# A router whose weight matrix becomes the stationary operand, with its logits turned back by small transposes

## The reference

```python
h = _layernorm(x) * (1 + cb) + sb               # x: 4 x 1024 x 256, after attention
probs = softmax(h @ Wr)                         # Wr: 256 x 8 experts
topk_probs, topk_experts = top_k(probs, 2)
for e in range(8):                              # at most 1280 tokens for each expert
    vals, idx = top_k(gate_of_expert_e, 1280)
    y = y.at[idx].add(g[:, None] * (relu(h[idx] @ W1[e]) @ W2[e]))
```

## Time and profile before

| | before |
|---|---|
| median of three runs | 1213.57 us |
| profiled execution, its own time | 1209.35 us |
| its span | 1207.5 us |
| TensorE busy | 1129.0 us (93%) |
| VectorE busy | 816.3 us (68%) |
| ScalarE busy | 420.4 us (35%) |
| GpSimd busy | 544.8 us (45%) |
| mean granted TensorE clock | 0.945 of full |

### The profile page before, as it was taken

The page is one execution under the profiler, slowest core; times in us unless marked ns, Lnnn a source line. Parts: engine busy times, 40 slices in busy tenths (PEclk is TensorE's granted clock), DMA queues, the critical chain, the costliest instruction groups (busy, mean ns, idle before and its releaser), DMA issues.

```text
span 1207.5 us, 17088 instructions
## 1 busy us (share of the span) xinstructions
PE 1129.0 (93%) x5810; PEld 980.5 (81%) x5810; DVE 816.3 (68%) x1549; ACT 420.4 (35%) x762; POOL 544.8 (45%) x403
## 2 busy tenths in 40 slices
PE   8998999999999999999985558999999999999996
PEld 5877888888888888887874447989898989899996
DVE  5587999589999999998476785444444444445442
ACT  5321122323223333231572202344353434444432
POOL 3220000377777777772000032666565657565723
PEclk9998999999999999999885558999999999999998
DMA  7110022433001111102441212754444353534322
GB/s 266 36 35 12 1 45 52 137 122 97 27 31 33 33 33 33 33 22 70 140 145 37 91 55 56 201 141 88 118 85 122 79 127 87 131 67 83 57 41 26
DMA packets 73985, 93.35 MB, mean 77 GB/s; under 512 B 5924, under 2 KB 61988, under 8 KB 73944
## 3 DMA queue, kind: packets, MB, share of 16 engines
q1 hardware_dynamic: 55928, 60.96, 16.3%
q0 software_dynamic: 18016, 31.86, 13.6%
HBM read 65.29 MB, written 23.31 MB: 73 GB/s over the span
## 4 chain that ended last, share of the span: by engine, by line
PE 73%; issue 13%; DVE 7%; ACT 2%; DMA 2%; POOL 2%; SPq 0%; DVEq 0%; POOLq 0%; ACTq 0%
PE ps L1459 27%; PE ps L1600 18%; PE ps L1616 12%; PE ps L1617 6%; PE ps L1487 2%; PE ps L1370 2%; DVE arena L1155 1%; PE ps L1582 1%; DMA qkv<-in_w 1%; DVE qkv L821 1%; PE ps L1562 1%; DVE arena_rounded L821 1%; PE ps L1545 1%; PE ps L1510 1%; ACT qkv L732 1%
## 5 line engine op out<-in xcount | busy, mean ns | idle before, releaser
L1600 PE MATMUL ps<-arena_rounded,w_high 128*128 128x384 f32 (+1 forms) x768 | 210.5, 355 | 2.1 <-DVE arena_rounded L821 2.1
L580 POOL TENSOR_TENSOR kv_low<-arena,kv_high 128x512 fp32r<-128x512 f32 x128 | 185.7, 1479 | 41.1 <-ACT kv_high L632 41.1
L1459 PE MATMUL ps<-kv_high,toep_high 128*128 128x512 f32 (+1 forms) x512 | 193.1, 377 | 1.0 <-POOL kv_low L580 1.0
L1459 PE MATMUL ps<-kv_low,toep_high 128*128 128x512 f32 (+1 forms) x512 | 193.1, 377 | 0.0
L1459 PE MATMUL ps<-kv_high,toep_low 128*128 128x512 f32 (+1 forms) x512 | 192.4, 376 | 0.0
L1272 DVE SCALAR_TENSOR_TENSOR hidden_low<-ps,hidden_high 128x384 fp32r<-128x384 f32 (+1 forms) x192 | 115.6, 602 | 98.9 <-ACT hidden_high L790 98.5
L604 POOL DMA_INDIRECT out<-arena x80 | 126.3, 1579 | 103.7 <-DVE arena L821 96.0
L593 POOL DMA_INDIRECT qkv<-row_scratch,arena x80 | 82.9, 1036 | 184.0 <-DVE arena L1226 158.0
L1600 PEld LDWEIGHTS ps<-arena_rounded,w_high 128*128 128x128 f32 x768 | 139.9, 189 | 13.2 <-issue 2.5
L790 ACT ACTIVATE hidden_high<-ps 128x384 fp32r<-128x384 f32 (+1 forms) x192 | 101.3, 528 | 125.6 <-PE ps L1600 125.6
L821 DVE TENSOR_TENSOR arena<-qkv 128x512 f32 (+1 forms) x128 | 133.3, 1099 | 7.2 <-DMA qkv<-arena 7.0
(11 more groups left out here) (198 smaller groups left out, 1971.9 us busy)
## 6 DMA issues: line engine op xcount, KB each, us to landing
arena<-ssm_scratch SPq DMA_DIRECT2D x32, 320.0 KB, 3.1
qkv<-in_w SPq DMA_DIRECT2D x16, 512.0 KB, 5.2
qkv<-in_w SPq DMA_DIRECT2D x8, 1024.0 KB, 10.7
arena<-in_u SPq DMA_DIRECT2D x7, 1024.0 KB, 6.2
row_scratch<-qkv SPq DMA_DIRECT2D x4, 1056.0 KB, 4.6
qkv<-arena SPq DMA_DIRECT2D x32, 128.0 KB, 2.4
row_scratch<-arena SPq DMA_DIRECT2D x4, 1024.0 KB, 6.4
out<-qkv SPq DMA_DIRECT2D x4, 1024.0 KB, 9.3
```

The source lines that it names most:

```text
L580: nc.gpsimd.tensor_tensor(kv_parts[s][1][:, quarter], kv_flat[s][:, quarter], kv_parts[s][0][:, quarter].bitcast(F32), ALU.subtract).then_ ...
L1459: last = mm(ps[:, 4 * s + g, (lo - 2 * g) * B * 64:BANK], toep_parts[s][a][:, o * P:(o + 1) * P], kv_parts[s][x][:, src], start=n == 0 and ...
L1600: last = mm(ps[:, f % 4, 0:width], w1_parts[q][a][:, dc * F + f * P:dc * F + (f + 1) * P], xeT_parts[x][dc][:, 0:width], start=dc == 0 and ...
```

## The change

The operands of the router are exchanged. `wr_sb` (128 features x 8 experts) is the stationary operand and the turned rows move, 512 tokens in each matmul, so a batch takes 4 matmuls, each writing 8 partitions x 512 tokens. The router now waits until all four pieces of `h2T` are there, where it waited for two and then for the other two. ScalarE copies the two halves into `logits_turned` (8 partitions x 1024) with `logits_out(b)`, which stands ahead of `normalize(b+1)`. TensorE turns them back with `logits_back(b)`, eight transposes of 8 x 128 to 128 x 8, which wait for both copies; from there VectorE reads them as before. logits_back(0) and logits_back(1) stand in the middle of attention_out(2) and attention_out(3), logits_back(2) ahead of router(3), logits_back(3) behind it.

```diff
-LOGIT_BANK = (2, 2, 0, 1)
+LOGIT_BANKS = ((2, 3), (2, 3), (0, 1), (4, 5))
...
+            def logits_out(b):
+                for half in range(2):
+                    act.wait_ge(turned_psum, 2 * b + half + 1)
+                    copy(logits_turned[0:E, half * BANK:(half + 1) * BANK],
+                         ps[0:E, LOGIT_BANKS[b][half], :]).then_inc(turned_copied, 1)
...
                 if b + 2 < B:
                     y_turned(b + 2)
+                logits_out(b)
                 if b + 1 < B:
                     normalize(b + 1)
...
                 for tb in range(TB):
+                    if tb == TB // 2 and b >= 2:
+                        logits_back(b - 2)
                     for cc in range(DC):
...
             def router(b):
+                pe.wait_ge(h2T_ready, 4 * b + 4)
+                if b == B - 1:
+                    pe.wait_ge(x2_ready, B)
+                for half in range(2):
+                    for cc in range(DC):
+                        last = mm(ps[0:E, LOGIT_BANKS[b][half], :], wr_sb[:, cc, :], h2T[b][:, cc, half * BANK:(half + 1) * BANK],
+                                  start=cc == 0, stop=cc == DC - 1)
+                    last.then_inc(turned_psum, 1)
+
+            def logits_back(b):
+                pe.wait_ge(turned_copied, 2 * b + 2)
                 for tb in range(TB):
-                    if tb % 4 == 0:
-                        pe.wait_ge(h2T_ready, 4 * b + tb // 2 + 2)
-                    for cc in range(DC):
-                        last = mm(ps[:, LOGIT_BANK[b], tb * E:(tb + 1) * E], h2T[b][:, cc, tb * P:(tb + 1) * P], wr_sb[:, cc, :],
-                                  start=cc == 0, stop=cc == DC - 1)
+                    last = transpose(ps[:, LOGIT_BANKS[b][0], tb * E:(tb + 1) * E], logits_turned[0:E, tb * P:(tb + 1) * P],
+                                     ident[0:E, 0:E])
                 last.then_inc(logit_psum, 1)
...
+                if b == B - 1:
+                    logits_back(b - 1)
                 router(b)
                 if b + 2 < B:
                     attention_out(b + 2)
+            logits_back(B - 1)
```

More of the change, by code:

```diff
@@ L207, in adaln_block @@
         ones_l = region(T0 + 1536, 256)
+        logits_turned = region(T0, 2 * BANK)
         junk = [region(T0 + start, 256) for start in (1792, 3072, 3328)]
@@ L313, in adaln_block @@
             sem(n) for n in ("w_high", "w_low", "xeT_high", "xeT_low", "hid_high", "hid_low"))
+        turned_psum, turned_copied = sem("turned_psum"), sem("turned_copied")
         waited, table_in, gates_out, rows_out, x2_out = (
@@ L1086, in centre_logits @@
                 dve.wait_ge(logit_psum, b + 1)
-                nc.vector.tensor_copy(row, ps[:, LOGIT_BANK[b], 0:TB * E].rearrange("p (t e) -> p t e", t=TB)).then_inc(logit_ready, 1)
+                nc.vector.tensor_copy(row, ps[:, LOGIT_BANKS[b][0], 0:TB * E].rearrange("p (t e) -> p t e", t=TB)).then_inc(logit_ready, 1)
                 dve.wait_ge(logit_ready, b + 1)
```

## The result

| | before | changed |
|---|---|---|
| median | 1213.05 us (9 runs, 1209.51 to 1213.73) | 1219.84 us (9 runs, 1217.11 to 1223.14) |
| profiled execution, its own time | 1209.35 us | 1220.16 us |
| its span | 1207.5 us | 1218.4 us |
| router(0) to the gates' turn, in the trace | 57.4 us (590.43 to 647.81) | 65.4 us (592.76 to 658.21) |
| start to router(0) | 590.4 us | 592.8 us |

The changed kernel is slower by 0.63%: the ratio is 1.0063 with an interval of 1.0051 to 1.0075, or 6.8 us between the medians. The stage of the router is 8.1 us longer. The 2.3 us ahead of it fall on identical instructions. From here on "the stage" is the time from the first router record to the gates' turn; where times of two kernels are compared, both are counted from router(0).

What follows compares the result with a forecast made beforehand. Bound: TensorE up to 621.8 us, then a latency chain through ScalarE and VectorE to the gates' turn at 647.81. +0.6, +1.1 and +5.5 make +7.2, with clock weighed +8: 1221.6 us on 1213.57; range 1216.5 to 1225.5.

Steps and rivals of the forecast that it cites:

- the sum: Delay at the exponential of batch 2: +0.6, +1.1 more and +5.5 more make +7.2 us.
- the clock weighed in: Half clock in part of router(2) would add 1.4 us; half of that weighed in gives +8.
- Step 1: Batch 0: TensorE gains 2.9 us, the clock staying full through router(0) and attention_out(2).
- Step 2: Batch 1: copies waiting for router(1) stand ahead of normalize(2) on ScalarE; its square root comes 0.6 us later.
- Step 3: Batch 2: the 1.28 us table load behind router(2)'s copy is no longer hidden; the square root comes 1.7 us late.
- Step 4: Batch 3: logits_out(3) makes the exponential of batch 2 wait for router(3), taken as 4.67 us; exponential 7.2 us later.
- The range: Whole time: 1216.5 us (+5.4 less 2 us between runs) to 1225.5 us (between +11 and +12.8).
- Rival of full clock throughout: TensorE holds full clock also in batch 3, router(3) takes 3.44 us: +5.4, 1219.0 us; chance 0.18.
- Rival of the clock lost as before: Routers run at half clock as before: up to +12.8, priced at +11, 1224.6 us; chance 0.17.
- Rival of a faster kernel: ScalarE's copies and table loads find cover, so the clock alone counts: -4.1, 1209.5 us; chance 0.05.
- the forecast's sign of 2 us: Sign of being wrong: a search or expert phase whose length changes by more than 2 us.

Runs made afterwards that it cites:

- the repeated run: The changed kernel measured once more, nothing altered, beside the kernel with early table loads; 1219.92 us, ratio 1.0068 to the kernel before.
- The filled kernel: The changed kernel plus five float32 matmuls of 512 columns, results unused, on TensorE ahead of h2_transposes(3); 1219.51 us, ratio 1.0057 to the kernel before.
- the best kernel: Against the kernel before: new form for batches 0 and 1, copies behind normalize(1) and normalize(2), logits_back(1) at three quarters of attention_out(3); 1208.35 us, ratio 0.9968.

## Why the prediction was right

The forecast was 1221.6 us, 8.0 over the 1213.57 of the three runs then shown; measured were 1219.84 and 6.8 over the 1213.05 of nine. The stage, which is what the steps speak of, became 8.1 us longer, where the sum says 7.2, and 8 with the clock weighed in. The mechanism was right at each step; that 8 meets 8.1 so closely is luck, since the 0.8 were put in for a half clock in router(2), which did not come, and were made up by router(3) and by a slower batch 0.

- Step 1 held, with a gain of 2.5 us where 2.9 was said. The clock stayed full, router(0) left TensorE after 3.53 us (592.76 to 596.29; 3.44 expected), logits_back took 0.59 (0.5 taken), and h2_transposes(1) stood at 11.3 us where 11.0 was expected.
- Step 2 held, larger: the square root of batch 2 is 22.2 us behind router(0), before 21.1. The loss is 1.0 us where 0.6 was expected, since router(1) started at 16.6 us instead of 16.2: the halves of attention_out(2) took 3.65 and 3.55 us, where 3.5 was taken, and router(0), logits_back(0) and the transposes ahead of router(1) 0.1 more each. The wait of h2_transposes(2) for VectorE is there, 1.83 us.
- Step 3 held. The table load follows the copy (630.11, 630.72, 632.01), and the square root of batch 3 is 2.1 us late, 1.7 expected; of these 0.4 are step 2's. No drain is seen here either: the load starts 0.6 us behind the start of a copy of 0.59 us, ends at 632.00, and the square root starts at 632.01. By the Trainium skill ("ScalarE: Activation LUTs", section on what ACT_TABLE_LOAD costs) a switch costs 1.38 us of drain besides the load. The measurement decides: there is no room for it here.
- Step 4 held; one term was undersized: router(3) took 5.25 us, not 4.67, as the clock was at half until 643.5 at least. These 0.6 us and the 0.4 of step 2 make up what the sum of 7.2 lacks. In the repeated run router(3) took 6.47 us and the stage 66.7, 9.3 over before: the term depends on where the clock comes back, and no run shows it at full clock.
- The clock in router(2), on which the weighing rested, was full in both traces of the changed kernel (3.60 us each).
- The range: +5.4 less 2 on 1213.57 gives 1217.0 for its lower end, not 1216.5. The measured time lies above both.
- Rival of full clock throughout: the clock stayed full through three routers but not through batch 3, as the forecast chose. The filled kernel shows that filling the idle time ahead of it wasn't enough. By the Trainium skill ("TensorE: Matmul & The Clock Gate", section "Why this matters for your kernels") a TensorE kept busy holds full clock. The trace agrees for batches 0 to 2 of the changed kernel. It doesn't in the kernel before, where TensorE's rows leave no gap from 590.43 us on and the clock is at half from 592.5.
- Rival of the clock lost as before: it failed for batches 0 to 2. For batch 3 it came near, with 6.47 of its 6.83 us for router(3) in the repeated run.
- Rival of a faster kernel: it named the exponential of batch 2 as the one point that decides. That is not enough: with the exponential ahead of router(3)'s end alone, 3.0 us of loss were left (1215.73 against 1212.76). Only where the copies leave the path of the normalizations too is the loss gone, and faster than before are only the kernels with the new form in one or two batches.

Why the medians moved by less than the stage (6.8 against 8.1 us) is not shown. The two profiled executions differ by 10.8 us, 2.3 of them ahead of router(0) and 0.5 behind the gates' turn, and the one of before is 3.7 us under the median; no trace of before at its median was kept. With the same instructions the time to router(0) went from 590.1 to 592.8 us in the twelve traces, and the time behind the gates' turn by 3.7 us, so the forecast's sign of 2 us there was too narrow (the changed kernel's two traces are 0.5 and 2.7 over before).

## What to carry to other kernels

When a result takes a new way through an engine that works in order, ask what stands behind the new instruction there: 1.2 us of copies for a batch lengthened the stage by 8, since two normalizations, three table loads and an exponential had to wait for a router of which they need nothing. Put such a copy behind what doesn't need it, and see where the compiler's table load lands; a one-element activation moves it. A gain of clock on TensorE is worth something only where TensorE's end is what the next engine waits for, which here holds for two batches of four: the best kernel has the new form in these two alone.

## What the runs showed that was not expected

- The exchange of operands bought nothing in matmul time: 3.53 us for eight records of 512 columns with 8 loaded, 3.50 for 32 records of 8 columns with 128 loaded, both at full clock but for the last 0.1 us of the latter. All that it bought was the clock.
- Eight transposes of 8 x 128 to 128 x 8 take TensorE 0.59 us (599.94 to 600.53) at full clock and 0.95 at half (639.51 to 640.46).
- Filling work kept TensorE's clock full where it stood, and bought no time in either experiment: in one the clock stayed at half longer in batch 1 (attention_out(3) 10.04 us, 8.8 before), in the other it fell just ahead of router(3).
- ScalarE's copy of 8 x 512 takes 0.59 us, as long as one of 128 x 512 (0.60 in the same trace): 8 partitions or 128 made no difference.
